# Windowed attention with a gated recurrence: every second quad masked by VectorE instead of TensorE, a reordered slot, and six batches of the last product moved ahead

## The chip, the cores and the metric

One core of a Trainium2 chip. The metric is the device time of one execution in microseconds (us). All times of the profile are of one profiled execution of the same program.

## The reference

Two parts, joined by a product at the end. Input `x` is 8 batches x 256 tokens x 128, fp32. `LN` is a layer normalisation with no scale and shift.

```
h   = LN(x)
u   = gelu(h W_u^T + b_u) * sigmoid(h W_g^T + b_g);   s_t = s_{t-1} A^T + u_t Bm^T;   y_t = s_t Cm^T + D
z   = h
for each of 6 layers:
    shift the upper half of z's channels by one token
    q, k, v = z Wqkv                    (16 heads of 64)
    q, k: l2-normalised per head, rotated by position
    attention in windows of 32 queries over 64 keys (own window and the one before), masked, softmax
    z = z + attention Wo
    shift again;  z = z + FFN(z)        (layer norm, 128 -> 2 x 341, a * gelu(gate), 341 -> 128)
out = x + y * silu(z)
```

The mask lets query i of a window see keys i to i+32 of its 64; in the first window the keys before the sequence are out.

## The kernel before, in words

**Steps and slots.** One pass of one batch through one layer is a step; there are 48 (6 layers x 8 batches, batches innermost). Every engine's program is a loop over steps, and in it over 8 slots, v0 to v7. Work of one step is spread over about five steps of the loop by lags: an item with lag L of a step's slot 0 runs L slots later (L44 to L53), so in steady state each slot holds work of several steps. The order of the work within a slot is the order of the statements in each engine's `step` (PE L506, ACT L706, VectorE L848, GpSimd L1015, SyncE L398); each engine executes its list in order, and semaphores tie the lists together. Nothing plans this at run time.

**Per slot.** One 128x512 projection for queries or keys, three fp32r matmuls (hi x hi, lo x hi, hi x lo; `project`, L499). ScalarE squares it (L712), VectorE multiplies it by two tables (L882, one read of PSUM, 1024 columns out; called t12 here), GpSimd adds the halves (L1052) and six slots later scales by the norm (L1027); TensorE transposes it (L544) and ScalarE copies it to QT or KT (L721). The projection of a slot waits for t12 of the slot before (L516), since both use the same PSUM bank.

**Per second slot ("quad": four head pairs' scores, 128x512).** Quads k0, k1, k2, k3 have their scores in v3, v5, v7 and v1 (lag 11): TensorE first writes the mask into both banks of `S2` by an identity product in bf16 (L554), then adds 64 small score products (L561). VectorE takes the maximum (L910) and subtracts it (L915), which also frees `S2`. In the even slot behind: ScalarE exp (L727), VectorE sum and reciprocal (L900, L904); then GpSimd multiplies (L1034, odd slot), TensorE transposes (L582), ScalarE copies (L737), TensorE multiplies with V (L636), ScalarE copies (L766). The V projection (L574), the transposes of a quad (L582) and the scores share `S2`, so each waits for the one before to be read.

**Newton.** In v1 and v5 VectorE computes reciprocal roots of the norms in 8 dependent instructions (L926 to L940), with two operands in `O2`, a bank that the product with V writes too: the product of v2 and v6 waits for it (L631), and so does GpSimd's scaling (L1024).

**Feed-forward.** Four groups of 8 matmuls with Wo in v5, v6, v7, v0 (L531), the residual sum xm in v0 (L867), three shift DMAs (L412 to L414), layer-norm statistics in v3 (L945), its GpSimd part in v4 (L1041 to L1047), a transposition in v5 (L610, called XT), an affine copy on ScalarE in v5 (L759), W1 in v0 and v1 (L662), gelu (L772), W2 in v3 (L601), xt in v4 (L965).

**Layer edges.** In the last step of a layer (slots v5, v6) and in the first of the next (v1, v2, v5, v7) six 128x512 blocks of new weights are rounded (ScalarE, L676) and split (GpSimd, L1009). VectorE makes new tables at the start of a layer (L854).

**The end.** After the last step: y is loaded back from HBM (L433), x is loaded again (L434), PE transposes y (L649), and for all eight batches ScalarE computes silu (L779), VectorE two products and sums (L975, L977), and the output goes out (L437).

The wait that ties the slots together:

```python
wait(pe, t12_done, g)                                   # L516, ahead of project()
wait(dve, sq_done, g + 1)                               # L879, ahead of L882
wait(pe, nw_seq, newtons_begun(s, v))                   # L631, ahead of L636
```

Of the kernel before, what the change touches and what calls it, by code (L numbers as in the profile page):

```python
# [15 lines left out]
P = 128  # L16
# [23 lines left out]
Y_SLOT = 12  # L40
Y_BACK = STEPS * SLOTS + 19
# [127 lines left out]
def gated_mix_kernel(nc, x, rec_w, rec_b, wqkv, wo, w1, w2, params, qk_scales, consts, y_spill, out):  # L169
    with ExitStack() as ctx:  # L170
# [61 lines left out]
        y_back = V[:, 1, 0:4, :].rearrange("p a b -> p (a b)").rearrange("p (b n) -> p b n", b=B)  # L232
# [43 lines left out]
        zeroed = sem("zeroed")  # L276
        s_ready, max_done, sub_done, exp_done = sem("s_ready"), sem("max_done"), sem("sub_done"), sem("exp_done")
# [62 lines left out]
        def _(sp):  # L340
# [57 lines left out]
            def step(s, par, b_):  # L398
                for v in range(SLOTS):
                    if LEAD <= s < LEAD + (DEPTH - 1) * B:  # L400
                        load_layer(s, v, b_)
                    if s * SLOTS + v == Y_SLOT:
# [28 lines left out]
            sp.wait_ge(y_saved, 16)  # L431
            sp.wait_ge(o_ready, QUADS)
            sp.dma_start(y_back, y_spill).then_inc(in_y, 16)  # L433
            sp.dma_start(x_tok, x.rearrange("b (t p) d -> p (b t) d", p=P)).then_inc(in_x2, 16)  # L434
# [8 lines left out]
        def _(pe):  # L443
# [62 lines left out]
            def step(s, par, b_):  # L506
                for v in range(SLOTS):
# [10 lines left out]

                    for k in range(QPS):
# [17 lines left out]
                    recurrence(in_fill(s, v, 0))  # L537

# [8 lines left out]
                    a, k, st, pr = quad(s, par, v, L_S)  # L547
# [19 lines left out]
                    u, vv, st, pr = unit(s, par, v, L_V)  # L567
                    if live(u, UNITS) and vv % 2 == 0:
# [4 lines left out]
                        wait(pe, sub_done, s_units(s, v))  # L573
                        project(V_ps, pr, c % 2, V_COLS[c // 2]).then_inc(v_ready, 1)  # L574

                    a, k, st, pr = quad(s, par, v, L_PT)
                    if live(a, QUADS):
                        wait(pe, p_norm, a + 1)
                        wait(pe, sub_done, upto(a + 2, QUADS))
                        wait(pe, pt_evac, a)  # L580
                        for ct in range(4):
                            mm = pe.transpose(PT_ps[:, P * ct:P * (ct + 1)], E[:, k, P * ct:P * (ct + 1)], ident)  # L582
                        mm.then_inc(pt_ready, 1)
# [9 lines left out]

                    f, pr = batch(s, par, v, F_W2)
# [9 lines left out]
                    f, pr = batch(s, par, v, F_XT)  # L604
                    if f is not None:
                        wait(pe, normed, (f + 1) * NT)
                        wait(pe, ff_final, f)
                        wait(pe, x_low, staged(s, v))
                        for t in range(NT):
                            mm = pe.transpose(BANK_XT[:, P * t:P * (t + 1)], xn[:, t, :], ident)  # L610
                        mm.then_inc(xnT_ready, 1)
# [3 lines left out]
                    f, pr = batch(s, par, v, F_W1)  # L615
                    if f is not None:
                        if f % B == 0:
                            wait(pe, in_w1, (f // B + 1) * 16)
                        wait(pe, xn_done, f + 1)
                        wait(pe, mid_done, begun(s, v, F_WO))  # L620
                        wait(pe, x_low, staged(s, v))
                        ff_w1(f, pr, [0, 1])
# [29 lines left out]
                    recurrence(in_fill(s, v, 1))  # L652
# [17 lines left out]
        def _(act):  # L670
# [35 lines left out]
            def step(s, par, b_):  # L706
                for v in range(SLOTS):
                    g = s * SLOTS + v
                    if live(g, UNITS):
# [15 lines left out]
                    if live(a, QUADS):  # L725
                        wait(act, sub_done, a + 1)
                        act.activation(E[:, k, :], E[:, k, :], ACT.Exp).then_inc(exp_done, 1)  # L727
# [399 lines left out]
```

## Time and profile before

| What | us |
|---|---|
| median of 3 runs (lowest to highest) | 1651.64 (1651.06 to 1654.09) |
| the profiled execution, its own time | 1658.21 |
| its span, first to last instruction | 1656.4 |
| busy: TensorE / VectorE / GpSimd / ScalarE | 1570.9 / 1419.4 / 1233.0 / 1110.8 |
| mean granted TensorE clock | 0.988 |

TensorE's busy time is modelled: the end of a matmul overlaps the next one, so start-to-start distances say more than durations. The time from one xm (L867) to the next is one step.

### The profile page before, as it was taken

How to read it: one execution, taken by the hardware profiler on the slowest of the kernel's cores; microseconds unless marked ns; L12 is line 12 of the kernel's file. 1: busy time of each engine (PE TensorE's matmuls, PEld its weight loads, DVE VectorE, ACT ScalarE, POOL GpSimd, SP SyncE). 2: the span in 40 equal slices, each digit the busy share in tenths (PEclk: the TensorE clock that was granted, in tenths of full speed). 3: DMA queues.
4: the chain of work that ended last, by engine and by line, in shares of the span. 5: the costliest groups of instructions: out<-in, count | busy, mean ns of one | idle time of the engine just before them, and what ended most of it. 6: DMA issues, size and time to landing. Idle time of an engine off the chain costs nothing.

```text
span 1656.4 us, 75425 instructions
## 1 busy us (share of the span) xinstructions
PE 1570.9 (95%) x31996; PEld 1315.8 (79%) x31996; DVE 1419.4 (86%) x2757; ACT 1110.8 (67%) x1980; POOL 1233.0 (74%) x1200
## 2 busy tenths in 40 slices
PE   5889999999999999999999999999999999999996
PEld 3467888788888788888888888788888878888875
DVE  5788999899889888989988988989899988989952
ACT  4266767777767776777766767776677776676762
POOL 2478788877778877777887777788777888777841
PEclk9799999999999999999999999999999999999997
DMA  3132223333223323222333322333322333322322
GB/s 112 28 96 69 68 72 85 86 83 81 69 69 84 90 66 94 70 69 72 96 76 75 86 68 69 93 79 82 82 68 70 95 79 79 81 69 66 74 58 80
DMA packets 109743, 127.96 MB, mean 77 GB/s; under 512 B 52065, under 2 KB 55649, under 8 KB 109153
## 3 DMA queue, kind: packets, MB, share of 16 engines
q1 hardware_dynamic: 109408, 123.13, 29.5%
q8 instruction: 256, 4.19, 1.1%
q14 instruction: 79, 0.64, 0.1%
HBM read 20.27 MB, written 2.10 MB: 14 GB/s over the span
## 4 chain that ended last, share of the span: by engine, by line
PE 61%; DVE 12%; ACT 11%; issue 8%; POOL 6%; DMA 1%; SPq 1%; DVEq 0%; POOLq 0%
PE F L531 10%; PE O L636 9%; PE VTb L544 7%; PE S L561 6%; PE QKb L502 6%; PE F L601 4%; PE QKb L504 4%; PE QKb L503 4%; DVE t L882 3%; ACT L772 3%; PE S L582 3%; DVE mx L910 2%; ACT hid L772 2%; POOL t L1052 2%; PE S L554 2%
## 5 line engine op out<-in xcount | busy, mean ns | idle before, releaser
L1052 POOL TENSOR_TENSOR t<-t 128x512 f32<-128x512 f32 x384 | 492.6, 1283 | 187.1 <-DVE t L882 173.8
L882 DVE TENSOR_TENSOR t<-QKb,table 128x1024 f32<-128x1024 f32 x384 | 468.4, 1220 | 62.1 <-ACT sq L712 60.0
L1027 POOL TENSOR_TENSOR t<-t,rn 128x512 f32<-128x512 f32 x384 | 401.9, 1047 | 128.7 <-DVE rn L939 128.7
L712 ACT ACTIVATE sq<-QKb 128x512 f32<-128x512 f32 x384 | 231.4, 603 | 231.9 <-PE QKb L504 226.6
L636 PEld LDWEIGHTS O<-PT,V 64*64 64x64 f32 x12288 | 198.8, 135 | 57.8 <-issue 55.8
L636 PE MATMUL O<-PT,V 64*64 64x32 f32 x12288 | 218.7, 221 | 16.0 <-DVE rn L939 16.0
L891 DVE TENSOR_REDUCE ss<-sq 128x16 f32<-128x1024 f32 x192 | 232.0, 1208 | 0.0
L544 PE MATMUL VTb<-cst,t 128*128 128x128 f32 x1536 | 231.0, 273 | 0.2
L531 PEld LDWEIGHTS F<-wo_sb,OT 128*128 128x128 f32 x1536 | 202.1, 193 | 16.3
L1034 POOL TENSOR_TENSOR E<-E,rs 128x512 f32<-128x512 f32 x192 | 200.7, 1045 | 14.6 <-DVE rs L904 14.6
L544 PEld LDWEIGHTS VTb<-cst,t 128*128 128x128 f32 x1536 | 185.8, 141 | 31.3 <-POOL t L1027 3.0
L531 PE MATMUL F<-wo_sb,OT 128*128 128x128 f32 x1536 | 204.6, 277 | 0.0
L502 PE MATMUL QKb<-w_hi,x_hi 128*128 128x512 f32 x384 | 194.7, 507 | 10.0 <-DVE t L882 9.3
L561 PE MATMUL S<-KT,QT 64*32 64x64 f32 x12288 | 167.2, 224 | 6.1 <-issue 6.1
L561 PEld LDWEIGHTS S<-KT,QT 64*32 64x32 f32 x12288 | 135.0, 105 | 46.9 <-issue 46.8
L910 DVE TENSOR_REDUCE mx<-S 128x8 f32<-128x512 f32 x192 | 131.7, 686 | 38.9 <-PE S L561 37.0
L721 ACT COPY KT<-VTb 128x512 f32<-128x512 f32 x192 | 112.2, 585 | 72.1 <-PE VTb L544 72.1
L721 ACT COPY QT<-VTb 128x512 f32<-128x512 f32 x192 | 113.4, 591 | 67.9 <-PE VTb L544 67.9
L504 PE MATMUL QKb<-w_hi,x_lo 128*128 128x512 f32 x384 | 152.9, 398 | 0.0
L503 PE MATMUL QKb<-w_lo,x_hi 128*128 128x512 f32 x384 | 152.6, 397 | 0.0
L915 DVE TENSOR_TENSOR E<-S,mx 128x512 f32<-128x512 f32 x192 | 132.8, 692 | 6.6
L900 DVE TENSOR_REDUCE sm<-E 128x8 f32<-128x512 f32 x192 | 129.9, 676 | 5.6 <-ACT E L727 5.5
(152 smaller groups left out, 2775.9 us busy)
## 6 DMA issues: line engine op xcount, KB each, us to landing
V<-v_tok SPq DMA_DIRECT2D x1440, 64.0 KB, 2.0
w_raw<-in_wqkv SPq DMA_DIRECT2D x36, 256.0 KB, 3.3
wo_sb<-in_wo SPq DMA_DIRECT2D x6, 512.0 KB
xs<-xm SPq DMA_DIRECT2D x48, 64.0 KB
xs<-xm SPq DMA_DIRECT2D x48, 63.5 KB
w_sb<-in_w SPq DMA_DIRECT2D x6, 341.0 KB, 3.4
w_sb<-in_w SPq DMA_DIRECT2D x6, 192.0 KB, 3.4
y_spill<-OT SPq DMA_DIRECT2D x1, 1024.0 KB, 4.3
```

Source lines behind the costliest of these rows:

```text
L502: pe.matmul(out_, hi, w_hi[:, col:col + 512], start=True, stop=False)
L504: return pe.matmul(out_, lo, w_hi[:, col:col + 512], start=False, stop=True)
L531: mm = pe.matmul(BANK_WO[:, D * t:D * (t + 1)], OT[:, pr, h, P * t:P * (t + 1)], wo_sb[:, h, :], start=(h == 0 and t == 0), stop=(h == HP ...
L544: mm = pe.transpose(VT_ps[:, P * i:P * (i + 1)], t12[:, vv, P * i:P * (i + 1)], ident)
L561: mm = pe.matmul(S2[WIN * w:WIN * (w + 1), p, KEYS * ct:KEYS * (ct + 1)], QT[64 * p:64 * (p + 1), 0, hp, tok:tok + WIN], KT[64 * p:64 * (p ...
L636: mm = pe.matmul(O2[64 * c:64 * (c + 1), p, WIN * w:WIN * (w + 1)], V[64 * p:64 * (p + 1), pr, w, hp * DH:(hp + 1) * DH], PT[64 * p:64 * ( ...
L712: act.activation(sq[:, v % 4, :], QK_ps, ACT.Square).then_inc(sq_done, 1)
L721: act.copy(to[:, pr, 4 * half:4 * half + 4, at:at + P], VT_ps.rearrange("p (i q) -> p i q", i=4)).then_inc(tr_evac, 1)
L882: dve.tensor_tensor(t12[:, v:9 + v % 4:8 + v % 4 - v, :].rearrange("p c (h d) -> p c h d", h=8), QK_ps.rearrange("p (h d) -> p h d", h=8). ...
L891: dve.tensor_reduce(ss[:, vv // 4, 8 * (vv % 4):8 * (vv % 4) + 16], sq[:, vv % 4:vv % 4 + 2, :].rearrange("p a (h d) -> p (a h) d", h=8), ...
L1027: pool.tensor_tensor(w, w, rn[:, vv // 4, 8 * (vv % 4):8 * (vv % 4 + 1)].unsqueeze(2) .to_broadcast([P, 8, DH]), ALU.mult).then_inc(qk_nor ...
L1052: pool.tensor_tensor(w, w, t12[:, 8 + v % 4, :].rearrange("p (h c d) -> p h c d", h=8, c=2)[:, :, ::-1, :], ALU.add).then_inc(add_done, 1)
```

## The change

Four parts.

1. **Mask.** For k1 and k3 the identity product with the mask is left out. VectorE adds the mask (from SBUF) while it reads the scores from PSUM into `E`, then takes the maximum from `E`; GpSimd subtracts the maximum in `E` one slot later, at the head of its even slots (v2 and v6), and ScalarE's exp waits for that. k0 and k2 stay as they were. `S2` is now released by `out_done`: for k1 and k3 after the addition.
2. **Order within the slots.** TensorE: XT moves from v5 to v6, behind the projection; the quad's transposes go ahead of the V projection; both ahead of the scores; W1 ahead of W2. ScalarE: the affine copy moves from v5 to the head of v0; V copy right behind exp; the gelus of v0 ahead of the PT copy. GpSimd: normalisation ahead of scaling; the layer-norm part moves from v4 to the end of v3, behind the addition; the weight splits go to the end of the slot. VectorE: scores' work right behind t12, statistics ahead of Newton, `stage_low` behind it. Recurrence pieces of the first slots are placed a little later in the lists.
3. **End.** y and x are loaded back during the last steps (into `sq` and `V`), silu and the two VectorE instructions of batches 0 to 5 run while the last batch's feed-forward is under way (at slots 402 and 405 of 432), and only batches 6 and 7 are left behind it.
4. The projections keep their three matmuls.

```diff
-L_S, L_EXP, L_NORM, L_PT, L_PV = 11, 12, 13, 14, 16
-F_WO, F_MID, F_SH, F_ST, F_NM, F_XT, F_AFF = 21, 24, 24, 27, 28, 29, 29
+L_S, L_SUB, L_EXP, L_NORM, L_PT, L_PV = 11, 12, 12, 13, 14, 16
+F_WO, F_MID, F_SH, F_ST, F_NM, F_XT, F_AFF = 21, 24, 24, 27, 27, 30, 32
+Y_LOAD, X_LOAD = STEPS * SLOTS + 4, STEPS * SLOTS + 8
+EARLY, GATED, MIXED = B - 2, STEPS * SLOTS + 18, STEPS * SLOTS + 21
-        y_back = V[:, 1, 0:4, :].rearrange("p a b -> p (a b)").rearrange("p (b n) -> p b n", b=B)
+        y_back = sq[:, :, :].rearrange("p a b -> p (a b)").rearrange("p (b n) -> p b n", b=B)
...
 TensorE, scores
-                        for p in range(2):
-                            pe.matmul(S2[:, p, 0:4 * KEYS], ident_bf[:, :], mask_bf[:, :], start=True, stop=False,
-                                      skip_group_check=True)
+                        masked = k % 2 == 0
+                        if masked:
+                            for p in range(2):
+                                pe.matmul(S2[:, p, 0:4 * KEYS], ident_bf[:, :], mask_bf[:, :], start=True, stop=False,
+                                          skip_group_check=True)
...
-                                                   start=False, stop=ct == 3, skip_group_check=True)
+                                                   start=not masked, stop=ct == 3 or not masked, skip_group_check=True)
...
 ScalarE, exp
-                        wait(act, sub_done, a + 1)
+                        if k % 2 == 0:
+                            wait(act, out_done, a + 1)
+                        else:
+                            wait(act, sub_done, a // 2 + 1)
...
 VectorE, scores
+                        else:
+                            wait(dve, pt_ready, a - 3)
+                            dve.tensor_tensor(Ek, Sv, cst[:, C_MASK:C_MASK + 4 * KEYS]
+                                              .rearrange("p (c k) -> p c k", k=KEYS).unsqueeze(1)
+                                              .to_broadcast([P, 2, 4, KEYS]), ALU.add).then_inc(out_done, 1)
+                            wait(dve, out_done, a + 1)
+                            dve.tensor_reduce(mv_, Ek, AX_X, ALU.max).then_inc(max_done, 1)
...
 GpSimd, head of the slot
+                    a, k, st, pr = quad(s, par, v, L_SUB)
+                    if live(a, QUADS) and k % 2 == 1:
+                        wait(pool, max_done, a + 1)
+                        w = E[:, k, :].rearrange("p (c b k) -> p b c k", c=4, b=2)
+                        pool.tensor_tensor(w, w, mx[:, k, :].rearrange("p (b c) -> p b c", b=2).unsqueeze(3)
+                                           .to_broadcast([P, 2, 4, KEYS]), ALU.subtract).then_inc(sub_done, 1)
...
 the order of the lists in a slot, by lag names
-PE:   QK, WO, rec, TR, S, V, PT, TX, W2, XT, W1[2], W1[0,1], PV, y, rec
+PE:   QK, XT, WO, TR, rec, PT, V, TX, S, W1[0,1], rec, W2, W1[2], PV, y
-ACT:  sq, TR, EXP, gelu[2], ROUND, PT, gelu[0,1], stage, V, AFF, PV
+ACT:  AFF, sq, TR, EXP, V, gelu[2], gelu[0,1], ROUND, PT, stage, PV
-POOL: SCALE, NORM, SPLIT, NM, add
+POOL: SUB, NORM, SCALE, add, NM, SPLIT
...
 the end
-            for b in range(B):
+                    if s * SLOTS + v == GATED:
+                        gate(range(EARLY))
+                    if s * SLOTS + v == MIXED:
+                        mix(range(EARLY))
+            gate(range(EARLY, B))
+            mix(range(EARLY, B))
```

## Rows read from the trace of the kernel before

**Rows 1.** The page: chain that ended last, by engine

```profile
PE 61%; DVE 12%; ACT 11%; issue 8%; POOL 6%; DMA 1%; SPq 1%; DVEq 0%; POOLq 0%
```

**Rows 2.** xm instructions; busy by stretch: a plain step, then a layer edge's two

```profile
L867 DVE TENSOR_TENSOR xm<-F,xt x48: 410/425/425, 129.7 to 1627.1; 128x256 f32<-128x256 f32 x48
838.26:869.99 31.73, 31.39 (x666) 26.79 (x665) 28.51 (x56) 22.42 (x40) 26.29 (x26) 1.00 0.28 68
1031.25:1064.96 33.71, 32.89 (x675) 27.89 (x673) 30.89 (x57) 24.80 (x45) 27.33 (x27) 1.00 0.34 85
1064.96:1097.93 32.97, 30.73 (x655) 25.61 (x656) 28.57 (x57) 23.04 (x42) 27.61 (x27) 1.00 0.37 96
```

**Rows 3.** Timeline of VectorE in the plain step: t12 of v1, of v5, k1's subtraction

```profile
844.16 1.23 DVE L882 TENSOR_TENSOR t<-QKb,table 128x1024 f32<-128x1024 f32 x1 [1.04 <-ACT sq L712]
...
859.11 1.23 DVE L882 TENSOR_TENSOR t<-QKb,table 128x1024 f32<-128x1024 f32 x1
...
861.12 0.69 DVE L915 TENSOR_TENSOR E<-S,mx 128x512 f32<-128x512 f32 x1
```

**Rows 4.** Timeline of TensorE there: product of v2, XT, projection of v6, v7's mask

```profile
848.56 1.14 PE L636 MATMUL O<-PT,V 64*64 64x32 f32 x64 [0.34 <-DVE rn L939]
...
860.28 0.44 PE L610 MATMUL F<-cst,xn 128*128 128x128 f32 x2
860.47 0.48 PE L502 MATMUL QKb<-w_hi,x_hi 128*128 128x512 f32 x1
...
866.99 0.38 PE L554 MATMUL S<-mask_bf,ident_bf 128*128 128x256 bf16 x2
867.30 0.86 PE L561 MATMUL S<-KT,QT 64*32 64x64 f32 x64
```

**Rows 5.** Timeline: a t12, and the projection that waits for its end

```profile
103.93 1.23 DVE L882 TENSOR_TENSOR t<-QKb,table 128x1024 f32<-128x1024 f32 x1 [0.54 <-ACT sq L712]
105.21 0.50 PE L502 MATMUL QKb<-w_hi,x_hi 128*128 128x512 f32 x1 [0.51 <-DVE t L882]
```

**Rows 6.** Groups of instructions: busy us, mean ns, idle time before

```profile
L915 DVE TENSOR_TENSOR E<-S,mx 128x512 f32<-128x512 f32 x192 | 132.8, 692 | 6.6
L1034 POOL TENSOR_TENSOR E<-E,rs 128x512 f32<-128x512 f32 x192 | 200.7, 1045 | 14.6 <-DVE rs L904 14.6
L1052 POOL TENSOR_TENSOR t<-t 128x512 f32<-128x512 f32 x384 | 492.6, 1283 | 187.1 <-DVE t L882 173.8
```

**Rows 7.** Timeline of GpSimd in the plain step, v4 and v6

```profile
857.96 1.28 POOL L1052 TENSOR_TENSOR t<-t 128x512 f32<-128x512 f32 x1
...
863.60 1.04 POOL L1027 TENSOR_TENSOR t<-t,rn 128x512 f32<-128x512 f32 x1 [1.12 <-DVE rn L939]
```

**Rows 8.** Timeline of ScalarE there: exp of k1, the square of v7

```profile
863.26 0.64 ACT L727 ACTIVATE E<-E 128x512 f32<-128x512 f32 x1
...
865.87 0.60 ACT L712 ACTIVATE sq<-QKb 128x512 f32<-128x512 f32 x1 [0.27 <-PE QKb L504]
```

**Rows 9.** Timeline at layer edges: a V projection held by a split; a split

```profile
830.74 0.50 PE L502 MATMUL S<-w_hi,x_hi 128*128 128x512 f32 x1 [1.07 <-POOL w_lo L1009]
```

**Rows 10.** The same view at another layer edge, GpSimd

```profile
1054.18 1.27 POOL L1009 TENSOR_TENSOR w_lo<-w_raw,w_hi 128x512 fp32r<-128x512 f32 x1
```

**Rows 11.** Timeline of the end, all engines

```profile
1635.71 1.58 POOL L1047 TENSOR_SCALAR xn<-xs,ln,rstd 128x128 f32<-128x128 f32 x2
...
1640.07 0.63 PE L610 MATMUL F<-cst,xn 128*128 128x128 f32 x2
...
1643.04 0.48 DVE L957 SCALAR_TENSOR_TENSOR hid<-F,prm,hid 128x256 f32<-128x256 f32 x1 [8.18 <-ACT hid L772]
...
1647.39 0.42 DVE L965 TENSOR_TENSOR xt<-F,xm 128x256 f32<-128x256 f32 x1 [1.70 <-PE F L601]
...
1653.73 0.43 DVE L977 TENSOR_TENSOR V<-xt,V 128x256 f32<-128x256 f32 x1
```

**Rows 12.** One line's instructions: duration in ns, min/median/max

```profile
L854 DVE TENSOR_TENSOR table<-cst,scales x12: 409/1232/2206, 36.4 to 1320.7; 128x256 f32<-128x256 f32 x12
```

More of the change, by code:

```diff
@@ L517, in step @@
                         project(QK_ps, par, tile, QK_COLS[2 * half + kind]).then_inc(qk_ready, 1)
+                    f, pr = batch(s, par, v, F_XT)
+                    if f is not None:
+                        wait(pe, normed, (f + 1) * NT)
+                        wait(pe, ff_final, f)
+                        wait(pe, x_low, staged(s, v))
+                        for t in range(NT):
+                            mm = pe.transpose(BANK_XT[:, P * t:P * (t + 1)], xn[:, t, :], ident)
+                        mm.then_inc(xnT_ready, 1)
                     for k in range(QPS):
@@ L545, in step @@
                         mm.then_inc(tr_ready, 1)
+                    recurrence(in_fill(s, v, 0))
+                    a, k, st, pr = quad(s, par, v, L_PT)
+                    if live(a, QUADS):
+                        wait(pe, p_norm, a + 1)
+                        wait(pe, out_done, upto(a + 2, QUADS))
+                        wait(pe, pt_evac, a)
+                        for ct in range(4):
+                            mm = pe.transpose(PT_ps[:, P * ct:P * (ct + 1)], E[:, k, P * ct:P * (ct + 1)], ident)
+                        mm.then_inc(pt_ready, 1)
+                    u, vv, st, pr = unit(s, par, v, L_V)
+                    if live(u, UNITS) and vv % 2 == 0:
+                        c = vv // 2
+                        if c % 2 == 0 and st % B == 0:
+                            wait(pe, lo_done[4 + c // 2], st // B + 1)
+                        wait(pe, v_evac, v_units(st, vv, 0) - 1)
+                        wait(pe, out_done, s_units(s, v))
+                        project(V_ps, pr, c % 2, V_COLS[c // 2]).then_inc(v_ready, 1)
+                    if v == TX and live(s + 1, STEPS):
+                        wait(pe, ff_final, s + 2 - B)
+                        wait(pe, ff_final, begun(s, v, F_W2))
+                        wait(pe, xn_done, begun(s, v, F_XT))
+                        for t in range(NT):
+                            mm = pe.transpose(BANK_TX[:, P * t:P * (t + 1)], xt[:, (s + 1) % B, t, :], ident)
+                        mm.then_inc(tx_ready, 1)
                     a, k, st, pr = quad(s, par, v, L_S)
@@ L708, in step @@
                     g = s * SLOTS + v
+                    f, pr = batch(s, par, v, F_AFF)
+                    if f is not None:
+                        if f % B == 0:
+                            wait(act, in_prm, (f // B + 1) * 16)
+                        wait(act, xnT_ready, f + 1)
+                        wait(act, w1_ready, f * NCH)
+                        act.activation(xc[:, :], BANK_XT[:, 0:N], ACT.Identity, bias=prm[:, f // B % 2, R_B:R_B + 1],
+                                       scale=prm[:, f // B % 2, R_G:R_G + 1]).then_inc(xn_done, 1)
                     if live(g, UNITS):
@@ L940, in step @@
                                                      op1=ALU.mult).then_inc(nw_seq, 1)
[L941 to L949 removed]
+                    if v == TX and live(s + 1, STEPS):
+                        stage_low(BANK_TX[:, 0:N], 1 - par, 2 * (s + 1))
+                    if s * SLOTS + v == MIXED:
+                        mix(range(EARLY))
             def hidden(f, par, chunks):
@@ L959, in hidden, with mix @@
                                              op0=ALU.add, op1=ALU.mult).then_inc(hid_done, 1)
+            def mix(batches):
+                dve.wait_ge(yT_ready, 1)
+                dve.wait_ge(in_x2, 16)
+                for b in batches:
+                    dve.wait_ge(g_done, b + 1)
+                    y_ = banks[b // 2][:, N * (b % 2):N * (b % 2 + 1)].rearrange("p (t d) -> p t d", t=NT)
+                    dve.tensor_tensor(xt[:, b, :, :], y_, xt[:, b, :, :], ALU.mult).then_inc(prod_done, 1)
+                    dve.wait_ge(prod_done, b + 1)
+                    dve.tensor_tensor(o_tok[:, NT * b:NT * (b + 1), :], xt[:, b, :, :], x_tok[:, NT * b:NT * (b + 1), :],
+                                      ALU.add).then_inc(o_done, 1)
             def finish(f, par):
@@ L1048, in step @@
                                 .then_inc(normed, 1)
-                    if live(g, UNITS):
-                        wait(pool, t12_done, g + 1)
-                        w = t12[:, v, :].rearrange("p (h c d) -> p h c d", h=8, c=2)
-                        pool.tensor_tensor(w, w, t12[:, 8 + v % 4, :].rearrange("p (h c d) -> p h c d", h=8, c=2)[:, :, ::-1, :],
-                                           ALU.add).then_inc(add_done, 1)
+                    for l, c in splits(s, v, b_, SPLIT):
+                        split_weights(l, c)
             all_steps(pool, step)
```

179 lines of the change are left out of this document (69 added, 110 removed).

## The prediction

> **What bounds the kernel now.** I read the page's chain first, then the distance from one xm to the next, then one plain step line by line. The chain gives TensorE 61%, VectorE 12%, ScalarE 11%, GpSimd 6% [rows 1]. That looks like a TensorE bound, but it is an average over slots with different limits. The steps repeat with great regularity: of the 45 distances between the first 46 of the 48 xm, 26 lie between 31.7 and 31.9 us, ten are the five pairs of about 33.7 and 33.0 us at the layer edges (16 us over plain steps in all), and seven are 32.1 to 33.6 us [rows 2]. In the plain step VectorE is busy 28.51 of 31.73 us, GpSimd 26.29, TensorE 31.39 by its modelled ends [rows 2].
>
> Two chains of nearly one length close the loop. The first is TensorE's from the product of v2 (848.56, itself held 0.34 us by Newton [rows 4]) to the projection of v1, then the square and t12 of v1, then maximum, subtraction, Newton, and the next product of v2. The second begins at the same t12 of v1 (844.16): from there VectorE has no idle time until t12 of v5 ends, 859.11 + 1.23 = 860.34 [rows 3]. The projection of v6 has to wait for that end. A projection that really waits starts 105.21 - (103.93 + 1.23) = 0.05 us behind it [rows 5], so here it could start at 860.39. It starts at 860.47 [rows 4]. TensorE is the limit by 0.08 us. That is all that TensorE alone can win up to this point.
>
> **The change, part by part.** *Mask product.* The two products and the start of the scores lie 867.30 - 866.99 = 0.31 us apart [rows 4]; 96 pairs go, 30 us of TensorE's time if all counted. For k3 (v1) nothing counts: maximum and subtraction follow t12 of v1, which ends at 845.39, when the scores are done, and the product of v2 waits for Newton anyhow; its wait grows from 0.34 to some 0.6 us. For k1 (v5) the scores end 0.2 to 0.3 us earlier, and the projection of v6 then waits for t12: worth 0.08 us at most.
>
> *VectorE.* The addition replaces the subtraction, the same form with one PSUM operand, 0.69 us [rows 6]; the maximum moves behind it. Sum zero, so the stretch from 844.16 to 860.34 keeps its 16.2 us. `S2` is free 0.7 us earlier for k1 and k3, which no row waits for.
>
> *XT behind the projection of v6.* XT used the time in which TensorE was waiting or nearly so; 860.47 - 860.28 = 0.19 us [rows 4]. Behind the projection it is paid in full. Projection of v6: 860.39 (-0.08), everything from Wo of v6 on: +0.11 us. From there to the square of v1 the list is the same work (transposes and V projection only change places), so a plain step takes 31.73 + 0.11 = 31.84 us. Over the 26 and the two at the ends, 28 steps: +3.1 us. In the seven longer ones TensorE stood still early in the step, VectorE has slack, and there the mask counts: 7 x -0.2 = -1.4 us.
>
> *GpSimd's subtraction.* Nearest rows: 1.045 us for one full operand and a broadcast one, which is this form, and 1.283 for two full ones [rows 6]; I take 1.05, with the upper end for the range. Two a step raise GpSimd from 26.3 to 28.4 us. In v2 it fits into the idle time before the scaling. In v6 the layer-norm part, now ahead of two scalings and two additions, pushes it: that part ends about 857.6 us (it ended at 857.96, ahead of v4's addition [rows 7]), then scale, add, normalise, scale, add at 1.00 or 1.24 us start to start gives 863.1, subtraction until 864.2; the scaling that waits for Newton started at 863.60 [rows 7] and comes at 864.2. Exp of k1 goes from 863.26 to 864.2, and behind it in ScalarE's list stand three copies and the square of v7. They take about 2.0 us, so the square could start at 866.2 against 865.87 before [rows 8]; it needs 866.0 anyhow for the projection. t12 of v7 ends about 868.1, and the projection of v0 gets there at 868.2 by TensorE alone. Cost 0 in a plain step, cover 0.1 us; at 1.28 us the cover is gone and it costs 0.15 to 0.2 us a step, 6 us in all.
>
> The Trainium skill, "GPSIMD Engine Reference", Engine selection, speaks against it: it advises VectorE for elementwise work and calls GpSimd about two times slower for two-input operations. The rows bear out the direction (692 against 1045 ns [rows 6]), and by that rule the sum would still be the one above, as the subtraction costs only by its place in the queue.
>
> *Layer edges.* A split takes 1.27 us [rows 10]. In the last step of a layer the first split (v5) now stands behind v5's addition and so directly ahead of the subtraction, and ScalarE's rounding of v6 stands between the V copy and the PT copy. The subtraction ends at 1058.3 by that step's clock, exp, V copy, rounding and two copies follow, and the square of v7 slips from 1058.8 to about 1061, t12 with it; VectorE's tables and xm come 1.8 us later. In the first step of the next layer the V projection of v6 waited 1.07 us for its split already [rows 9]. The split now follows v5's addition and more work: wait +1.0 us, less the 0.43 us of transposes that go ahead of V: about +0.6. Together +2.4, five times: +12 us. Bounds: 0 (the longer waits fall into slack that the tables leave) and +4 us an edge.
>
> *The end.* Before, xn was ready at 1635.71 + 1.58 = 1637.3 but XT started at 1640.07, behind y's load and 16 transposes [rows 11]. With y loaded early these go ahead, so XT starts at 1637.4: -2.7 us. The two instructions of six batches (12 of 16, from 1647.7 to 1654.2, 6.4 us [rows 11]) leave the tail: 12 x 0.40 = -4.8 us. They run before `hid` of the last batch; y's transposes end about 1636, so they fill VectorE until about 1641 where `hid` could start at 1637.4 + (1643.04 - 1640.07) = 1640.4: +0.5 us. The new loads (1 MB each) sit in SyncE's queue ahead of V moves and shift DMAs that have 3 us of room. End: -7.0 us, bounds -5 and -8. VectorE's sums with both operands in SBUF run beside GpSimd's xn; the table sums of the same kind lasted 409 to 2206 ns [rows 12], so the tail's +0.5 could be +2. The Trainium skill ("SBUF — State Buffer", the section on engine ports) says that such a sum and a GpSimd instruction exclude each other for a whole instruction; the trace agrees by that spread.
>
> *The start.* Reordered recurrence pieces: 0, between -1 and +1 us.
>
> **Sum.** 3.1 - 1.4 + 12 - 7.0 = +6.7 us, against the profiled execution's own time 1658.21 (span 1656.4): 1664.9. The median of the runs lies 6.6 us below that execution; I take the same difference: 1651.64 + 6.7 = 1658.3.
>
> **Rivals.** *TensorE is the bound after all* (other side, faster). The place is the projection of v6: if VectorE passes t12 of v5 early enough, the mask of k1 counts 0.2 to 0.3 us in every step. It decides from 0.3 us of slack on VectorE between v1 and v5. For it: TensorE 61% of the chain, a few steps with such slack. Against it: no VectorE idle row there in any plain step. Time: over 42 steps -0.25 + 0.19 each is -2.5 us, and -10 us if XT is covered too; edges +2, end -7: 7.5 to 15 us below 1651.6, say 1640.
>
> *Only the end counts.* The steps come out alike, edges too (bounds above); XT and the mask cancel, and some 6 us of edges meet the end's 7: 1651.6 + 6 - 7 = 1651, no change.
>
> *GpSimd becomes the bound.* 1.28 us for the subtraction and a late exp in each step: 0.2 x 35 = 7 us, and edges at +4 in place of +2.4, 8 us more: 1658.3 + 15 = 1673.
>
> **How the numbers follow.** 0.2% is 3.3 us, about what a measurement here can tell from no change. My forecast, with +10 to +20 us of steps and edges before the end's gain: 0.42; GpSimd the bound: 0.12; only the end counts: 0.20; TensorE the bound: 0.26. Slower 0.53, same 0.20, faster 0.27. The range takes in the upper part of the faster case and most of GpSimd's: 1639 to 1672. Since both signs hold much of the chance: the forecast's own range is 1654 to 1665.
>
> **What would show it.** Right: plain steps of 31.8 to 31.9 us; the projection of v6 waiting 0.2 to 0.4 us for t12 of v5; the product of v2 waiting about 0.6 us for Newton; exp of k1 waiting for GpSimd; edges of about 35.5 and 33.6 us; last xt near 1645 by the old clock and 2 us from there to the last sum. Wrong: plain steps below 31.7 us with VectorE idle between v1 and v5; edges no longer than before; a subtraction on GpSimd above 1.2 us.

## The result, and the profile after

The changed kernel takes 1664.46 us (median of 4 runs, 1663.21 to 1666.74), the kernel before beside it 1652.16 (1651.06 to 1654.09). The ratio is 1.0071, 95% interval [1.0055, 1.0087]: slower by 0.7%, or 9.1 to 14.4 us. The profiled execution after took 1663.68 us (span 1661.9), close to its median; the one before (1658.21, span 1656.4) lay 6 us above its own. So the two traces differ by only 5.5 us, and some of the difference between the medians can't be placed in them.

The page of the changed kernel, busy time by engine and the chain that ended last (before: [rows 1]):

```profile
PE 1554.1 (94%) x31804; PEld 1290.5 (78%) x31804; DVE 1422.5 (86%) x2757; ACT 1099.0 (66%) x1982; POOL 1332.3 (80%) x1296
...
PE 37%; DVE 26%; issue 14%; ACT 12%; POOL 8%; DMA 1%; SPq 0%; POOLq 0%; DVEq 0%; ACTq 0%
```

GpSimd has 99 us more work, TensorE 17 us less, and TensorE's share of the chain fell from 61% to 37%. Busy time by stretch, with the columns of [rows 2]: a plain step, and both steps of a layer edge.

```profile
846.61:878.47 31.86, 31.28 (x662) 26.39 (x661) 28.60 (x56) 22.07 (x40) 27.43 (x28) 1.00 0.29 71
1038.30:1073.67 35.37, 32.81 (x671) 27.35 (x669) 31.11 (x58) 24.50 (x45) 29.80 (x29) 1.00 0.34 83
1073.67:1106.95 33.28, 30.59 (x651) 25.24 (x652) 28.64 (x56) 22.95 (x42) 29.91 (x29) 1.00 0.35 92
```

The median plain step went from 31.74 to 31.87 us, the last step of a layer from 33.7 to 35.36, the first of the next from 32.95 to 33.28. In sums: the five edges +10.0 us, the other 33 inner steps +2.9 (both traces hold some long ones of 32.3 to 33.6 us, at other places in each execution), first and last -0.4; from the 46th xm to the 48th -2.7 (that stretch lasts between 44.5 and 48.8 us in the fourteen traces of this case, in no order that goes with the kernel; before it took 48.4, after 45.7); from there to the last sum -4.9; the start +0.5. Together +5.4.

The timeline of a plain step (from 846.61), where TensorE and VectorE meet and where GpSimd hands on k1:

```profile
856.88 1.14 PE L648 MATMUL O<-PT,V 64*64 64x32 f32 x64 [0.55 <-DVE rn L975]
...
867.43 1.23 DVE L903 TENSOR_TENSOR t<-QKb,table 128x1024 f32<-128x1024 f32 x1
867.82 0.86 PE L607 MATMUL S<-KT,QT 64*32 64x64 f32 x64
868.71 0.50 PE L510 MATMUL QKb<-w_hi,x_hi 128*128 128x512 f32 x1
...
871.43 1.05 POOL L1059 TENSOR_TENSOR E<-E,mx 128x512 f32<-128x512 f32 x1
872.51 0.63 ACT L749 ACTIVATE E<-E 128x512 f32<-128x512 f32 x1 [0.67 <-POOL E L1059]
```

The product of v2 waits 0.55 us for Newton (0.34 before [rows 4]). t12 of v5 ends at 868.66 and the projection of v6 starts at 868.71, at the 0.05 us that a waiting projection has [rows 5]. The scores of k1 seem to last until 868.68, but that end is modelled. From the start of a quad's scores to the start of what follows them it is 0.79 us where nothing is waited for, and 0.89 here, so the projection waited 0.10 us. And this step is an exception: in v3 TensorE had lost 0.2 us (859.50 to 860.51 from the scores to W2, 1.01 in place of 0.79). In 27 of the 33 inner steps the distance ahead of the projection of v6 is 1.0 us or more, with a median of 1.06, so the projection usually waits 0.27 us for t12. Such a step, in which t12 ends at 964.46:

```profile
963.45 0.86 PE L607 MATMUL S<-KT,QT 64*32 64x64 f32 x64
964.51 0.50 PE L510 MATMUL QKb<-w_hi,x_hi 128*128 128x512 f32 x1 [0.20 <-DVE t L903]
```

(The bracket counts from the modelled end.) The exp of k1 waits for GpSimd. The waits of the whole execution (us in total, times, longest):

```profile
ACT E L749 <- POOL E L1059: 42.1, 47, 2.2
PE O L648 <- DVE rn L975: 26.1, 47, 0.7
PE QKb L510 <- DVE t L903: 25.4, 49, 2.0
```

The groups of the new instructions (columns of [rows 6]): the subtraction on GpSimd, the addition and the maximum on VectorE.

```profile
L1059 POOL TENSOR_TENSOR E<-E,mx 128x512 f32<-128x512 f32 x96 | 100.3, 1045 | 9.8 <-DVE mx L929 8.7
L929 DVE TENSOR_REDUCE mx<-E 128x8 f32<-128x512 f32 x96 | 65.9, 686 | 3.3
L925 DVE TENSOR_TENSOR E<-S,cst 128x512 f32<-128x512 f32 x96 | 65.8, 685 | 10.3 <-PE S L607 9.9
```

The end. First the timeline of the changed kernel, then its busy time over the last W1 (the first product of the last feed-forward), and then the same view of the kernel before over its own last W1.

```profile
1637.40 0.42 DVE L884 TENSOR_TENSOR xm<-F,xt 128x256 f32<-128x256 f32 x1 [6.32 <-PE F L547]
...
1646.01 2.01 POOL L1091 TENSOR_SCALAR xn<-xs,ln,rstd 128x128 f32<-128x128 f32 x2
...
1648.08 0.69 PE L533 MATMUL F<-cst,xn 128*128 128x128 f32 x2 [2.44 <-POOL xn L1091]
...
1650.43 1.06 PE L674 MATMUL F<-xc,w_sb 128*128 128x256 f32 x2
1651.29 1.06 PE L673 MATMUL F<-xc,w_sb 128*128 128x256 f32 x2
...
1657.63 0.42 DVE L1007 TENSOR_TENSOR xt<-F,xm 128x256 f32<-128x256 f32 x1 [1.70 <-PE F L629]
...
1659.21 0.42 DVE L1000 TENSOR_TENSOR V<-xt,V 128x256 f32<-128x256 f32 x1
```

```profile
1648.00:1655.00 7.00, 6.18 (x14) 3.87 (x14) 3.39 (x9) 2.85 (x5) 0.02 (x1) 0.51 0.31 94
```

```profile
1640.00:1647.00 7.00, 5.05 (x27) 3.53 (x26) 1.45 (x3) 3.78 (x7) 0.00 (x0) 0.94 0.00 0
```

From the last xm, XT comes after 10.68 us (before 13.0), which is 2.3 us gained (0.4 less than if xn had taken the 1.58 us of before [rows 11] in place of 2.01); from XT to xt it takes 9.55 us (before 7.32 [rows 11]), 2.2 us lost; from xt to the last sum 1.58 (before 6.34), 4.8 gained. The loss in the middle has its row: in 1648 to 1655 the granted clock was 0.51, so TensorE ran at 1.2 GHz, and the groups of W1 started 0.86 us apart. TensorE had waited 2.44 us for xn ahead of XT. Before, with a granted clock of 0.94 over the 7 us around the last W1, groups started 0.43 to 0.50 us apart; there the transposes of y had kept TensorE busy (though at 0.58 in part).

### The profile page after: what moved, and what is told of

Read it like the earlier page. It is cut to its first block, busy times and chain, and to the rows that moved or that the text cites. A ratio compares the mean times of both kernels' runs of the same rounds, so it can differ in the third digit from the quotient of the medians.

```text
span 1661.9 us, 75140 instructions
## 1 busy us (share of the span) xinstructions
PE 1554.1 (94%) x31804; PEld 1290.5 (78%) x31804; DVE 1422.5 (86%) x2757; ACT 1099.0 (66%) x1982; POOL 1332.3 (80%) x1296
## 4 chain that ended last, share of the span: by engine, by line
PE 37%; DVE 26%; issue 14%; ACT 12%; POOL 8%; DMA 1%; SPq 0%; POOLq 0%; DVEq 0%; ACTq 0%
DVE t L903 9%; PE F L547 7%; PE O L648 4%; PE QKb L510 4%; PE VTb L558 4%; PE S L607 3%; ACT L795 3%; DVE sm L940 3%; DVE ss L933 2%; PE QKb L512 2%; PE QKb L511 2%; POOL t L1080 2%; ACT hid L795 2%; ACT sq L731 2%; DVE E L925 2%
## 5 line engine op out<-in xcount | busy, mean ns | idle before, releaser
L547 PEld LDWEIGHTS F<-wo_sb,OT 128*128 128x128 f32 x1536 | 196.8, 191 | 12.8
L749 ACT ACTIVATE E<-E 128x512 f32<-128x512 f32 x192 | 121.9, 635 | 45.7 <-POOL E L1059 42.1
L780 ACT COPY OT<-O 128x512 f32<-128x512 f32 x192 | 114.5, 596 | 5.6 <-PE O L648 3.5
```

Source lines behind the costliest of these rows:

```text
L547: mm = pe.matmul(BANK_WO[:, D * t:D * (t + 1)], OT[:, pr, h, P * t:P * (t + 1)], wo_sb[:, h, :], start=(h == 0 and t == 0), stop=(h == HP ...
```

## Experiments

All ratios are to the kernel before, in runs on the same chip; one per mille is 1.65 us. "Edge" is the sum of a layer's last step and the next one's first (66.6 before, 68.6 after); "plain" is the clean step that repeats most (31.73, 31.86).

| Kernel | median us | ratio [95%] | plain | edge |
|---|---|---|---|---|
| before + mask | 1660.32 | 1.0043 [1.0031, 1.0055] | 31.66 | 68.4 |
| before + end | 1647.66 | 0.9965 [0.9952, 0.9978] | 31.74 | 66.8 |
| after, old mask | 1661.52 | 1.0053 [1.0038, 1.0068] | 31.87 | 67.45 |
| after, XT in v5 | 1658.40 | 1.0034 [1.0022, 1.0046] | 31.75 | 68.6 |
| before, no mask product | 1649.03 | 0.9975 [0.9965, 0.9985] | 31.67 | 66.5 |
| after, splits later | 1667.80 | 1.0093 [1.0079, 1.0108] | 31.87 | 70.2 |
| after, rounding last | 1664.51 | 1.0071 [1.0058, 1.0085] | 31.87 | 68.5 |
| before + end, TensorE kept busy | 1647.07 | 0.9968 [0.9956, 0.9980] | 31.74 | 66.6 |
| after, scales in PSUM | 1658.38 | 1.0043 [1.0031, 1.0055] | 31.87 | 67.55 |
| before + end, scales in PSUM | 1643.46 | 0.9949 [0.9936, 0.9961] | 31.74 | 65.5 |
| before, maximum of k3 twice | 1681.17 | 1.0177 [1.0164, 1.0190] | 32.46 | 67.4 |
| before + end + PSUM + mask away from edges | 1643.89 | 0.9945 [0.9932, 0.9959] | 31.66 | 65.5 |

**What sets a plain step.** The kernel before, with the maximum of k3 taken a second time:

```diff
+                        if k == 3:
+                            dve.tensor_reduce(mv_, Sv, AX_X, ALU.max).then_inc(dup_done, 1)
+                            wait(dve, dup_done, a // 4 + 1)
```

> The kernel before with the maximum of k3 (v1) taken twice on VectorE, the second behind the first, same result: 0.70 us more once a step, inside the stretch from t12 of v1 to t12 of v5. By the prediction's reading of the kernel before (VectorE has no idle time there, TensorE reaches the projection of v6 only 0.08 us later): plain steps 31.73 + 0.70 - 0.08 = 32.35, between 32.2 and 32.45 us, total +20 to +30 us. Rival 'TensorE is the bound': the second maximum falls into slack, plain steps up by less than 0.25 us, total +10 us or less.

```profile
1015.32:1047.78 32.46, 31.63 (x666) 26.81 (x665) 29.20 (x56) 22.53 (x40) 24.71 (x25) 1.00 0.29 70
```

+0.73 us a step and +29 us in all: a VectorE instruction at that place is paid in full. It is paid on both chains, though. The second maximum stands ahead of Newton too, so the product of v2 comes later with it (its wait for Newton is 0.34 us as before), and the projection of v6 still starts 0.15 us behind the end of t12 in the median, as in the kernel before. I had expected the 0.08 us by which TensorE is late to be taken off; this is why they were not, and why this run alone doesn't tell the two chains apart from that product on; what it excludes is a loop of TensorE alone. The opposite, TensorE relieved and nothing added (`masked = k % 2 == 0` ahead of the product, and `start`, `stop` as in the change; the scores of k1 and k3 stay unmasked):

> The kernel before with the mask's identity product left out for k1 and k3 and nothing in its place (those scores stay unmasked): the pure saving on TensorE, with no instruction more on any engine. My theory, after the run with part 1 alone had plain steps of 31.66 us: the product is worth what VectorE's stretch leaves, 0.05 to 0.1 us a plain step, and at the layer edges 0 to 0.2 us; plain steps 31.63 to 31.70 us, total -1 to -4 us against before. Rival 'TensorE is the bound, and what part 1 adds on the other engines hid it': plain steps shorter by 0.25 to 0.6 us, total -10 us or lower.

The 0.31 us of the product [rows 4] gave 0.06 us a plain step, and the projection of v6 now starts 0.06 us behind t12 in place of 0.15: the 0.08 us of the prediction are gained, and the rest of the saving is spent waiting. Total -4.1 us [-5.8, -2.5], a little beyond what I expected; 28 x 0.06 and 0.1 to 0.2 an edge make 2.5 of it. TensorE as the bound is out.

**The mask alone**, in the old order:

```diff
+                        masked = k % 2 == 0
...
+                            dve.tensor_tensor(Ek, Sv, cst[:, C_MASK:C_MASK + 4 * KEYS]
...
+                    a, k, st, pr = quad(s, par, v, L_SUB)
+                    if live(a, QUADS) and k % 2 == 1:
+                        wait(pool, max_done, a + 1)
```

> The kernel before with part 1 of the change alone: k1 and k3 without the identity product, VectorE adds the mask, GpSimd subtracts at the head of v2 and v6; order of the lists and end as before. My theory (VectorE's unbroken stretch from t12 of v1 to t12 of v5 sets the step, so the product of the mask is hidden): plain steps 31.65 to 31.75 us against 31.73, the two steps of a layer edge together longer by 0 to 1.5 us, total -3 to +5 us against before. Rival 'TensorE is the bound': plain steps shorter by 0.25 us or more, total -10 us or lower. Rival 'GpSimd becomes the bound': plain steps longer by 0.15 us or more, total +6 us or higher.

```profile
873.48:905.14 31.66, 31.10 (x662) 26.42 (x661) 28.49 (x55) 22.31 (x40) 26.79 (x27) 1.00 0.33 85
1065.76:1100.31 34.55, 30.97 (x656) 25.65 (x655) 28.58 (x57) 23.53 (x44) 30.60 (x30) 1.00 0.36 94
```

The plain step came as said, and edges and total did not: the total is +7.1 us, more than I gave it, as the rival with GpSimd had it, but without its longer plain steps. The edges carry all of it, 1.8 us each (10 us in the trace in all), nearly all in the first step of a layer (32.95 to 34.6). Its timeline shows a split, an addition and then the subtraction on GpSimd, with ScalarE waiting:

```profile
1073.54 1.29 POOL L1023 TENSOR_TENSOR w_lo<-w_raw,w_hi 128x512 fp32r<-128x512 f32 x1 [2.88 <-ACT w_hi L679]
1074.78 1.27 POOL L1072 TENSOR_TENSOR t<-t 128x512 f32<-128x512 f32 x1
1076.02 1.04 POOL L1039 TENSOR_TENSOR E<-E,mx 128x512 f32<-128x512 f32 x1
...
1077.09 0.63 ACT L733 ACTIVATE E<-E 128x512 f32<-128x512 f32 x1 [1.36 <-POOL E L1039]
```

**The mask taken back, in the new order** (`masked = True`, VectorE subtracts in every quad, no subtraction on GpSimd):

> The changed kernel with part 1 taken back alone: all four quads get the identity product and VectorE subtracts the maximum, nothing on GpSimd; new order and new end stay. My theory: at the layer edges the exp of k1 no longer waits for a split and a subtraction on GpSimd, so the pair of edge steps is 1 to 2 us shorter than in the changed kernel (68.65 us), -5 to -9 us in all; in plain steps the trace of the changed kernel shows TensorE and VectorE reaching the projection of v6 within 0.05 us of each other, so the product comes back on the path: plain steps +0.1 to +0.3 us, +4 to +10 us in all; total against the changed kernel -5 to +4 us. Rival 'TensorE is the bound': plain steps +0.3 to +0.6 us and edges no shorter, total +12 us or more over the changed kernel. Rival 'GpSimd is the bound': plain steps and edges both shorter, total -8 us or lower.

Plain steps did not grow (31.87 against 31.86): the product of the mask is hidden here too, where I had expected it back on the path. It fits into the wait ahead of the projection of v6: from the start of k1's scores to that projection it is now 0.85 us in the median, in place of 1.06. The edge is 1.2 us shorter, the last step of a layer alone 1.0 us, one subtraction. So of the edge's +2.0 us the mask makes 1.2, and the order 0.8. By the medians the mask costs about 3 us in the new order (between -0.6 and 6.6, so it can't be told from nothing) and 7 in the old one.

**XT back in v5**, behind W2 in TensorE's list (`F_XT` 30 to 29):

> The changed kernel with XT back in v5, behind W2 in TensorE's list, as before. As the prediction had it (behind the projection of v6 it is paid in full, 0.19 us, ahead of it it is covered by the wait for t12 of v5): plain steps 0.1 to 0.2 us shorter than the changed kernel's, total -4 to -7 us against it. Rival, from the changed kernel's trace (projection of v6 starts 0.05 us behind t12, so nothing is left to cover XT): plain steps within 0.05 us, total within 2 us of the changed kernel.

-6.1 us [-9.4, -2.8] against the changed kernel, plain steps 31.75. The first expectation holds. The rival came from one step of the changed kernel's trace, the exception named above; in most of the others the projection waits 0.27 us, and that is the cover. In front of the projection XT fits into it wholly: from the start of k1's scores to the projection it is 1.06 us with XT between them and 1.06 without. Behind the projection it costs 0.12 of its 0.19 us. The run also shows what I had put at nothing: with XT back in its place the plain step is still 31.75 us, against 31.66 with the mask's change in the old order. The rest of the new order costs 0.09 us a step.

**Order at the edges.** Two moves in the changed kernel. The first:

```diff
-ROUND, SPLIT = 2, 2
+ROUND, SPLIT = [2] * 6, [3, 3, 2, 2, 2, 2]
```

> The changed kernel with the splits of the first two weight blocks of a layer one slot later (v6 and v7 in place of v5 and v6), so that no split stands between t12 of v5 and GpSimd's subtraction of k1 in the last step of a layer. My theory: the subtraction and exp of k1 come about 1.2 us earlier there, the last step of a layer falls from 35.36 us to between 34.3 and 34.7 us, the first step of the next stays at 33.3 us, total -3.5 to -5.5 us against the changed kernel. Rival 'the edge is longer by the new order of the lists (rounding ahead of the PT copy), not by the subtraction's place': the last step stays within 0.3 us of 35.36 us, total within 1.5 us of the changed kernel.

The second, from ahead of the PT copy to the end of ScalarE's slot:

```diff
-                    for l, c in splits(s, v, b_, ROUND):
-                        round_weights(l, c)
...
+                    for l, c in splits(s, v, b_, ROUND):
+                        round_weights(l, c)
```

> The changed kernel with the rounding of weights at the end of ScalarE's slot, behind the copies of PT and OT. My theory: in the last step of a layer the rounding of v6 (0.61 us) leaves the way between the V copy and the square of v7, the step falls by 0.4 to 0.7 us to about 34.8 us; in the first step of the next layer the split of v5 waits for its rounding longer and the V projection of v6 with it, +0 to +0.6 us; total -4 to +1 us against the changed kernel. Rival 'only the split ahead of the subtraction matters': last step unchanged at 35.36 us, total +0 to +3 us.

The second gave the numbers that were expected (last step 34.74, next 33.79, nothing in total), and not for the reason expected. At the end of v6 the rounding still stands ahead of the square of v7: that square starts 29.64 us after the step's xm in both kernels, and the tables start 32.75 us after it in both. What fell is the time of the two table products themselves. In the changed kernel, then here:

```profile
1071.05 2.69 DVE L875 TENSOR_TENSOR table<-cst,scales 128x256 f32<-128x256 f32 x2
```

```profile
1068.20 1.27 POOL L1043 TENSOR_TENSOR w_lo<-w_raw,w_hi 128x512 fp32r<-128x512 f32 x1 [0.47 <-ACT w_hi L687]
1071.12 2.06 DVE L875 TENSOR_TENSOR table<-cst,scales 128x256 f32<-128x256 f32 x2
1071.44 1.46 POOL L1080 TENSOR_TENSOR t<-t 128x512 f32<-128x512 f32 x1
```

The split waited 0.47 us for the later rounding, so GpSimd's addition stood 0.5 us later beside the tables. The first product got through in 0.63 us in place of 2.36, and the addition took 1.46 us in place of 1.28.

The first run missed its expectation, and with that says most. (It is also slower in total: three of the five first steps of a layer took 34.9 to 36.2 us in place of 33.3. The second split now stands in v7; that it is the cause is not shown.) The subtraction came 1.26 us earlier in the step, and exp, the square of v7 and t12 with it, but at four of the five edges xm did not move; at the fifth the step took 34.30 us, as expected. VectorE and GpSimd in one of the four:

```profile
1073.22 0.69 DVE L921 TENSOR_TENSOR E<-S,mx 128x512 f32<-128x512 f32 x1
1073.82 3.96 DVE L875 TENSOR_TENSOR table<-cst,scales 128x256 f32<-128x256 f32 x2
1077.70 0.41 DVE L884 TENSOR_TENSOR xm<-F,xt 128x256 f32<-128x256 f32 x1
```

```profile
1072.64 1.04 POOL L1074 TENSOR_TENSOR t<-t,rn 128x512 f32<-128x512 f32 x1
1073.64 1.27 POOL L1080 TENSOR_TENSOR t<-t 128x512 f32<-128x512 f32 x1
1074.88 1.28 POOL L1043 TENSOR_TENSOR w_lo<-w_raw,w_hi 128x512 fp32r<-128x512 f32 x1
1076.12 1.04 POOL L1074 TENSOR_TENSOR t<-t,rn 128x512 f32<-128x512 f32 x1
```

The two table products took 3.96 us instead of 2.69 (0.41 each is the shortest [rows 12]) and ended only when GpSimd's unbroken row had: 1076.12 + 1.04 = 1077.16, xm 0.54 later. At the fifth edge the first product got through in 1.08 us. In the changed kernel xm follows GpSimd's row by 0.54 us at all five edges. So it does in the run with the old mask, and there t12 of v7 ends 1.9 us earlier than in the changed kernel, but GpSimd's row only 1.0 us, and xm comes 1.0 us earlier. So where the tables are shut out, GpSimd's backlog sets xm, and t12 does not.

**The scales in PSUM**, to test that (copied there by ScalarE, read by VectorE; TensorE's product with V waits for the tables, as it writes that bank):

```diff
+        scl_ps = O2[:, 1, N:N + 2 * DH].rearrange("p (k d) -> p k d", k=2)
+                    if v == SLOTS - 1 and b_ == B - 1 and s + 1 < STEPS:
+                        act.copy(scl_ps[:, :, :], scales[:, :, :]).then_inc(scl_ps_done, 1)
-                                          scales[:, kind, :].unsqueeze(1).to_broadcast([P, 2 * NT, DH]),
+                                          src[:, kind, :].unsqueeze(1).to_broadcast([P, 2 * NT, DH]),
+                        if v == 0 and b_ == 0 and s > 0:
+                            wait(pe, tab_done, 2 * (s // B + 1))
```

> The changed kernel, but VectorE's two table products at a layer's start read the scales from PSUM (ScalarE copies them there in v7 of the last step of the layer before) in place of SBUF; same result. Theory formed from the runs so far: in the last step of a layer xm comes 0.54 us behind the end of GpSimd's unbroken row of instructions in each of the four kernels looked at, since the table products with both operands in SBUF don't get through while GpSimd works; so the tables take 0.7 to 0.9 us in place of 2.69, the last step of a layer falls from 35.36 us to between 33.5 and 33.9 us, and part of that is given back in the next step by GpSimd's backlog: pair of edge steps -1 to -1.8 us, total -5 to -9 us against the changed kernel. Rival, the prediction's own chain (subtraction, exp, square of v7, t12 of v7 set xm): tables start at the same moment and take as long as they take, last step unchanged within 0.3 us, total within 2 us.

```profile
L887 DVE TENSOR_TENSOR table<-O,cst x10: 414/415/416, 289.4 to 1331.0; 128x256 f32<-128x256 f32 x10
```

```profile
1038.73:1072.25 33.52, 31.46 (x662) 26.48 (x661) 29.23 (x58) 23.18 (x43) 28.43 (x28) 1.00 0.33 83
1072.25:1106.28 34.03, 31.99 (x662) 26.63 (x661) 28.88 (x55) 24.02 (x44) 31.23 (x31) 1.00 0.37 97
```

All ten products now take 0.415 us, with GpSimd as busy as ever. The last step fell by 1.84 us, the next gave back 0.75, and the total is 4.6 us [1.3, 7.9] lower than the changed kernel's, a little less than expected. One sentence of the expectation was too wide: the 0.54 us hold in the changed kernel, with XT in v5, with the old mask and at four edges with the splits later. With the rounding last, and often in the old order, GpSimd's instruction beside the tables is the longer one instead (1.23 or 1.47 us in place of 1.04 and 1.27), so there both give way. And since the old kernel's tables took 2.2 to 2.6 us too, the stretch is a cost that both kernels carry, not the difference between them. That difference is seen once both are rid of it: the last step of a layer then takes 33.51 us here and 32.01 in the old order (the run with end and scales, below), since the tables start 32.75 us after xm here and 31.3 there, behind the later t12. So the prediction's chain is real, and it is what would be left.

**The end alone**, and with TensorE kept busy (idle transposes of the identity into a free bank, 20 behind y's and 8 behind the last XT):

> The kernel before with part 3 alone: y and x loaded back during the last steps, silu, product and sum of six batches ahead of the last batch's feed-forward. My theory: xm distances as before, last xm to last sum 26.7 us before and 20 to 22 us here, total -5 to -7 us. Rival 'the end is hidden or paid back' (loads collide with the moves of V, or the granted clock falls in the last feed-forward and takes the gain): total -2 to +1 us.

> The kernel before with part 3 alone (as in the run of that name) and besides 20 idle transposes on TensorE into a free bank behind the transposes of y and 8 behind the last XT, so that TensorE is busy until the last W1; nothing reads them. My theory: in that run the granted clock was at half while the last W1 groups ran (starts 0.85 us apart against 0.43), which ate part of the end's gain; with TensorE busy the last W1 runs at 0.43 us, last xm to last sum falls from 21.8 us to 19.5 to 20.3 us, total -7 to -8 us against before. Rival 'the clock falls there for another reason than the idle time', or 'the idle transposes delay XT': last xm to last sum 21.5 us or more, total -5 us or less gain.

The end alone gives 5.8 us. In its trace, as in the changed kernel's, last xm to last sum is 21.8 us, and the granted clock over its last W1 (1637 to 1643) was 0.55. With the idle transposes:

```profile
1636.00:1640.00 4.00, 2.61 (x15) 1.65 (x14) 1.45 (x3) 2.74 (x5) 0.00 (x0) 1.00 0.21 66
```

Full clock, and 19.5 us from xm to the last sum. But the ratios of the two kernels, 0.9965 and 0.9968, can't be told apart, the runs of each spread over 5 to 6 us, and the total of -7 to -8 us was missed. The clock's cost is shown in the traces; that runs without a profile pay it is not.

**Combinations:**

> The kernel before with part 3 (the end) and with the scales of the tables in PSUM, nothing else. By the table theory: tables 0.7 to 0.9 us in place of about 2.5, the last step of a layer from 33.7 us to 31.9 to 32.8 us, total against before: -5.5 us for the end and -4 to -8 us for the tables, -9 to -13 us. Rival 'the tables only fill time in which VectorE would wait': the end alone, -4 to -7 us.

> The kernel before with part 3 (the end), the scales of the tables in PSUM, and part 1 only where GpSimd's subtraction falls outside the last step of a layer and the first of the next (there VectorE subtracts and the mask's product stays); order of the lists as before. From the runs so far: plain steps 31.66 to 31.70 us in place of 31.73, edges as in the run with end and tables alone (31.95 and 33.45 us), so 1 to 3 us below that run: total -9 to -12 us against before. Rival 'GpSimd's subtraction costs in plain steps too': plain steps 31.8 us or more, total -6 us or less gain.

Both beat both kernels: 1643.46 us, 8.4 us below the kernel before [6.4, 10.6]. The tables' part was 2.6 us by the medians (between -0.4 and 5.7), less than I gave it; the trace has last steps of 32.0 and next steps of 33.45 in place of 32.95, so 1.2 us an edge, 6 us in all. The last run (`masked = not lite(a)`, where `lite` is true for k1 and k3 except where the subtraction would fall into an edge step) has the plain step of 31.66, no loss at the edges, and a ratio that can't be told from the run without a mask change. Its expected 1 to 3 us are neither shown nor excluded.

## Why the prediction was right, and where it was off

The forecast was slower, 1658.3 in 1639 to 1672; it came out at 1664.46.

- *What bounds a plain step*: right. TensorE has 0.08 us to win and no more (0.06 won by leaving out 0.31), and what is added on VectorE between t12 of v1 and Newton is paid one for one (+0.73 for +0.70).
- *Mask worth at most 0.08 us in v5*: 0.06 to 0.07 in the old order, 0.01 in the new.
- *The projection of v6 waits 0.2 to 0.4 us for t12 of v5*: right, 0.27 us in the median.
- *XT behind the projection costs 0.19, +0.11 net*: the sum was right (31.86 for 31.84), its parts were not. XT cost 0.12, between two kernels that differ in nothing else, and the rest of the order, put at nothing ("the list is the same work"), cost 0.09. That they made up for each other was luck. What in the order costs 0.09 stays open. Over all steps XT costs 6.1 us by the medians [2.8, 9.4], against 3.1 said: ten of the changed kernel's inner steps took 32.0 us, with XT in v5 three.
- *GpSimd's subtraction*: right at 1.045 us, and in its place. Exp of k1 was forecast for 25.9 us after the step's xm and started at 872.51 - 846.61 = 25.90. Cost in a plain step 0.
- *Layer edges +2.4 (+1.8, +0.6)*: measured +2.0 (+1.66, +0.33). The chain to the square of v7 and t12 held: both come 2.0 us later (2.2 said), and the tables start 1.5 us later. The last link was wrong: the tables' own time was taken as fixed, and in the changed kernel they wait for GpSimd's row, so t12 could come 1.3 us earlier without moving xm. That the step still came out at nearly the size said is luck in part. Of its +1.66 us the subtraction makes 1.0, by way of GpSimd's row, and the other 0.6 goes with the new order. The prediction put that down to the rounding ahead of the square of v7; the run meant to test it left the rounding ahead of that square, so this stays open.
- *The seven longer steps -1.4*: not seen. Steps of 32.3 to 35 us come in every execution at other places; what makes them stays open.
- *End -7.0*: -4.9 in the trace, -5.8 by medians. XT came 2.3 us earlier (2.7 said; xn was 0.4 us longer beside VectorE's sums), the 12 instructions left 4.8 us (4.8 said), and the +0.5 for a busy VectorE did not come. The step that failed is the silent one, that the last W1 would run as before: the granted clock fell to 0.51 over it, 2.2 us.
- *Sum*: +6.7 said, +12.3 [9.1, 14.4] measured, at the upper end of the forecast's own 1654 to 1665. XT's 3 us more, the 1.4 that did not come and the end's 1.2, less 2 us at the edges, make 3.6 of the 5.6 us between them; 2 us stay open, within the interval.
- *Rivals*: TensorE as the bound is excluded by two runs. GpSimd as the bound is wrong in plain steps and, at the edges, half right: its row sets xm there, but an edge costs 2.0 us and not 4.

## What to carry to other kernels

Where two engines meet once a step, two small runs say more than the shares of the chain: leave out an instruction on the one, and double one on the other. Before the second, look which chains the doubled instruction stands on; here it stood on both. Then measure the meeting over all steps, by distances from start to start. One step showed both engines arriving together, and it was an exception: the usual one had 0.27 us of waiting, which is what hid a piece in front of the meeting and not behind it. A transfer of work to an engine with room on average is paid where its queue is already full: here five layer edges cost more than the plain steps gained. And a number that comes out as said still needs its reason looked up: the rounding moved to the end gave the 0.6 us expected by another way.

## What the runs showed of the hardware

- A VectorE product with both operands in SBUF, 0.41 us at its shortest, took up to 3.6 us while GpSimd had instructions one behind the other. Which engine gives way differs. At all five edges of the changed kernel the first product ended only behind GpSimd's row; with the rounding last it got through in 0.63 us, and GpSimd's addition beside the tables took 1.46 us in place of 1.28. With one operand in PSUM the product took 0.415 us in ten of ten. The Trainium skill ("SBUF — State Buffer", the section on SBUF's two separate sides) says that such an instruction and a GpSimd instruction exclude each other for a whole instruction. The trace agrees for VectorE and goes further: in the last step of a layer with the splits moved the product was shut out for the rest of one instruction and two whole ones behind it. On GpSimd's side the delay was only about 0.2 us, less than the 0.41 us of a product.
- The same pair shows at the end: GpSimd's two xn took 2.01 us beside VectorE's sums, and 1.58 before [rows 11].
- TensorE had waited 2.4 us ahead of XT, and from 1648 to 1655 us the granted clock was 0.51; with TensorE kept busy it was 1.00 over the last W1.
